# One program for both attentions and the networks between them, with each network twist in two column halves

## The chip, the core and the metric

The kernel runs on one core of a Trainium2 chip. Five engines work side by side: TensorE (PE; matmuls, transposes, and loads of weights, PEld), VectorE (DVE), ScalarE (ACT), GpSimd (POOL) and SyncE (SP), which here issues all DMAs. Each engine takes its own instructions in program order and waits on semaphores that the others raise. The metric is the device time of one execution in microseconds (us); lower is better.

## What is computed

Two layers on x of shape (4, 1024, 128) in float32. Each adds to x the product of an attention s and a gate silu(g). The first attention is full with 16 heads of 8, the second is causal with a bias by position (ALiBi). The first gate comes from a squared-ReLU network and five steps of a spiking neuron; the second from a small coupling network that is run three times over, each time with a "twist" of the state.

```python
    x = L0_attn_x
    xn = _layernorm(x, axis=-1)
    s = _L0_attn_ref(xn, ...)                 # full attention, residual xn
    g = _silu(_L0_ffn_ref(xn, W_fc, W_proj))  # relu^2, W_proj, five spiking steps
    x = x + s * g
    xn = _layernorm(x, axis=-1)
    s = _L1_attn_ref(xn, ...)                 # causal attention with ALiBi
    g = _silu(_L1_ffn_ref(xn, ...))
    x = x + s * g

    def _L1_ffn_ref(x, ...):
        gf = _global_net(x.mean(axis=1, keepdims=True), ...)
        out = x
        for _ in range(NUM_CYCLES):           # 3
            tf = _coupling_net(out, ...)      # gelu, gelu, gelu, sigmoid: 128-128-64-32-1
            combined = 0.7 * gf + 0.3 * tf
            coupling = BASE_COUPLING + adaptive_range * (combined - 0.5) * 2.0
            out = out + coupling * _twist(out)
        return out

    def _twist(x):
        o_r, o_i, p_r, p_i = jnp.split(x, 4, axis=-1)
        return jnp.concatenate([p_r, -p_i, -o_r, o_i], axis=-1)
```

## The kernel before

The kernel is written by hand, engine by engine; the order of the text is the order on each engine. It consists of six programs one behind the other (`prologue`, `row_maxima` for layer 0, `first_attention`, `middle`, `row_maxima` for layer 1, `second_attention`). Each is an `nc.Block()`: at its end all five engines meet at a barrier.

**Attention.** Both attentions go through the batches (4), pairs of head groups, query halves and key tiles in steps. In a step TensorE makes the scores of four heads (128 keys by up to 512 queries each, `a_sc`), ScalarE takes the Exp of them in two instructions of 128x1024 (L979 in the first attention, L1846 in the second), and TensorE multiplies with the values into `a_o` (L1193, L2032). Scores live in three slots of two PSUM banks, the exponentials in a ring of four buffers (`probs`, `RING = 4`), so that step t of ScalarE waits for the product of step t - 4 (`pv_done`). The product of step 0 stands on TensorE behind the scores of step 3. In the second attention GpSimd zeroes the masked triangle of the diagonal steps (L1872) before the product. Before the first product VectorE clears `a_o` (L1155, L1948) and raises `o_clear`; TensorE waits for that ahead of its first score.

**Networks.** `middle` runs the coupling network on x, held transposed in `y` (channels by tokens). Two streams of two batches each take turns: six rounds n = 0 to 5 (stream n mod 2, cycle n // 2). A round on TensorE is `first_layer(n,0)`, `last_layer(n-1)`, `first_layer(n,1)`, `second_layer(n,0)`, `second_layer(n,1)`, `third_layer(n)` (lines 1585, 1613, 1585, 1592, 1592, 1600); ScalarE takes the Gelus (L1397) and, behind the last layer, the Tanhs of the sigmoid (L1418), one of 128x1024 for each of the stream's two batches k. The twist of a batch is three VectorE instructions over all 1024 columns: two of 64 partitions (L1517), each making one half of the rows of `change` from the other half of the state, and one of 128 partitions (L1520) that adds it to the state:

```python
for dst, src in ((low_half, high_half), (high_half, low_half)):
    ins = nc.vector.scalar_tensor_tensor(moved[dst, :], t[src, :], offset[...], out[src, :], ALU.add, ALU.mult)
links.after(ins)
nc.vector.scalar_tensor_tensor(out, moved, slope[:, 0:1], out, ALU.mult, ALU.add).then_inc(twisted[z], 1)
```

`first_layer(n,k)`, two matmuls of 512 columns, waits for the whole twist of round n-2. In rounds 0 and 1 `middle` also does the second half of batch 3 ("31" in the names), which the first attention left over: its output projection (L1654), update and normalization on VectorE (L1541 to L816; L1541 is the first of them), its transpose (L1632), and the queries and keys of both halves. The queries, keys, values and norms of the half "31" (L1636, L1640, L1647) are made in round 5; VectorE makes from the norms the flag (L1569 to L1575) that says whether the second attention needs exact row maxima. With these inputs it doesn't, so `row_maxima` of layer 1 loads the flag on TensorE, VectorE and SyncE, and each jumps over its body. VectorE starts `middle` with some twenty small instructions on constants (L1502 to L1539). In front of its first Gelu and behind its last Tanh ScalarE loads another function table (ACT_TABLE_LOAD at L1446 and L1477).

## Time and profile before

| | us |
|---|---|
| median of 3 runs (916.01 to 917.1) | 916.91 |
| the profiled execution | 914.3 |
| its span from first to last instruction | 912.6 |
| ACT busy in the span | 829.2 (91%) |
| PE busy in the span | 780.9 (86%) |
| DVE busy in the span | 395.0 (43%) |
| POOL busy in the span | 210.3 (23%) |
| mean granted TensorE clock, of full speed | 0.975 |

Stages by the timeline, in us from the span's start: prologue to 50.9, first attention from 55.9 (first Exp) to 534.2 (last), networks and what stands between up to 621.8 (first Exp of the second attention), second attention to the end. A busy share is a mean over stages with different limits; in the stage of the networks no engine is full. A row's times are those of one profiled execution, and the end of a matmul is modelled.

### The profile page before, as it was taken

The page shows a single profiled execution, that of the slowest core. Times are in us where ns is not written, and L with a number is a line of the kernel's source. Part 1 is how long each engine was busy: PE and PEld are TensorE (multiplying, and loading weights), DVE is VectorE, ACT ScalarE, POOL GpSimd, SP SyncE. Part 2 cuts the span into 40 slices and gives each one's busy share as a digit, 9 for nine tenths or more (in the row PEclk, how much of TensorE's full clock was granted, in tenths as well). Part 3 has the DMA queues.
Part 4 walks back from the last instruction along what each step waited for, and adds up shares of the span by engine and source line. Part 5 has one row for each costly group of instructions (what it writes and reads, how often), then busy time and mean ns, then how long its engine had stood idle before and what let it go on. Part 6 is the DMA issues. An engine that isn't in the chain of part 4 may idle for free. (4 is left out here: it accounts for less than half of the span.)

```text
span 912.6 us, 22160 instructions
## 1 busy us (share of the span) xinstructions
PE 780.9 (86%) x9374; PEld 305.5 (33%) x9374; DVE 395.0 (43%) x862; ACT 829.2 (91%) x919; POOL 210.3 (23%) x259
## 2 busy tenths in 40 slices
PE   3949999899999999998999988755887878878876
PEld 2412434234343343433334333212332323323322
DVE  7821254443747446474444777881120121121122
ACT  7759999999999999999999956656999999999996
POOL 2201110130202212121311112002234334324333
PEclk9969999999999999999999999986999999999999
DMA  6882020200300202103000034010112022022000
GB/s 181 281 280 38 2 75 3 74 2 3 98 25 18 104 2 75 48 2 121 2 2 24 25 90 168 0 47 1 38 38 86 14 74 86 1 87 86 2 13 24
DMA packets 31948, 53.45 MB, mean 59 GB/s; under 512 B 5480, under 2 KB 16360, under 8 KB 31848
## 3 DMA queue, kind: packets, MB, share of 16 engines
q1 hardware_dynamic: 31848, 52.01, 18.2%
q8 instruction: 75, 1.23, 0.6%
q14 instruction: 25, 0.20, 0.1%
HBM read 31.29 MB, written 20.71 MB: 57 GB/s over the span
## 5 line engine op out<-in xcount | busy, mean ns | idle before, releaser
L979 ACT ACTIVATE a_probs<-a_sc 128x1024 f32<-128x1024 f32 x512 | 473.6, 1035 | 10.0 <-PE a_sc L1178 9.7
L1846 ACT ACTIVATE a_probs<-a_sc 128x1024 f32<-128x1024 f32 x288 | 269.6, 1047 | 21.6 <-PE a_sc L1997 17.1
L1193 PE MATMUL a_o<-a_probs,vt 128*18 128x256 f32 (+1 forms) x3072 | 271.3, 456 | 0.0
L1178 PE MATMUL a_sc<-q_st,k_st 32*128 32x512 f32 x1024 | 130.7, 499 | 29.5 <-ACT a_probs L979 23.4
L2032 PE MATMUL a_o<-a_probs,vt 128*18 128x256 f32 (+3 forms) x1856 | 152.7, 437 | 0.7
L1991 PE MATMUL a_sc<-q_st,k_st 32*128 32x512 f32 (+3 forms) x768 | 78.5, 423 | 62.5 <-ACT a_probs L1846 51.1
L1872 POOL TENSOR_SCALAR_AFFINE_SELECT a_probs<-a_probs 128x512 f32<-128x512 f32 x128 | 82.8, 666 | 189.9 <-ACT a_probs L1846 189.9
L1193 PEld LDWEIGHTS a_o<-a_probs,vt 128*18 128x18 f32 x3072 | 65.2, 97 | 142.9 <-issue 102.7
L1178 PEld LDWEIGHTS a_sc<-q_st,k_st 32*128 32x128 f32 x1024 | 50.6, 183 | 145.4 <-ACT a_probs L979 135.4
L1006 POOL TENSOR_TENSOR early<-early 128x512 f32<-128x512 f32 x32 | 38.4, 1200 | 176.9 <-DVE early L1116 176.9
L1991 PEld LDWEIGHTS a_sc<-q_st,k_st 32*128 32x128 f32 x768 | 37.1, 185 | 123.8 <-ACT a_probs L1846 106.5
L1905 DVE STREAM_TRANSPOSE a_turn<-a_o 128x512 f32<-128x512 f32 x15 | 10.8, 717 | 152.9 <-PE a_o L2032 152.9
L2032 PEld LDWEIGHTS a_o<-a_probs,vt 128*18 128x18 f32 x1856 | 40.6, 97 | 69.4 <-issue 51.2
L1116 DVE TENSOR_SCALAR early<-a_side 128x512 f32<-128x512 f32 x32 | 22.1, 691 | 67.0 <-PE a_side L112 67.0
L1120 DVE TENSOR_SCALAR y<-a_side,rho 128x128 f32<-128x128 f32 x32 | 9.0, 345 | 92.5 <-PE a_side L112 92.5
L992 POOL TENSOR_TENSOR early<-early,y 128x512 f32<-128x512 f32 x7 | 10.6, 1513 | 144.5 <-DVE early L1131 144.5
L1397 ACT ACTIVATE n_h<-n_ps,cn_b 128x1024 f32<-128x1024 f32 (+1 forms) x24 | 24.1, 1006 | 20.5 <-PE n_ps L1585 10.3
L1517 DVE SCALAR_TENSOR_TENSOR early<-n_th,n_offset,y 64x1024 f32<-64x1024 f32 x24 | 30.8, 1285 | 8.6 <-ACT n_th L1418 8.2
L1014 POOL TENSOR_TENSOR a_square<-parts 128x512 bf16<-128x512 f32 x12 | 15.1, 1258 | 82.7 <-DVE parts L1148 82.7
L112 PE MATMUL a_side<-proj_t,early 128*32 128x128 f32 x1024 | 33.8, 273 | 0.0
L112 PE MATMUL a_side<-y,fc_t 128*32 128x512 f32 x256 | 33.3, 592 | 0.0
L112 PEld LDWEIGHTS a_side<-proj_t,early 128*32 128x32 f32 x1024 | 29.3, 110 | 5.8
(236 smaller groups left out, 712.9 us busy)
## 6 DMA issues: line engine op xcount, KB each, us to landing
q_st<-q_hl SPq DMA_DIRECT2D x48, 256.0 KB
k_st<-k_hl SPq DMA_DIRECT2D x48, 256.0 KB
q_hl<-parts SPq DMA_DIRECT2D x12, 512.0 KB, 4.3
k_hl<-parts SPq DMA_DIRECT2D x12, 512.0 KB, 4.5
q_hl<-early SPq DMA_DIRECT2D x4, 512.0 KB, 4.8
k_hl<-early SPq DMA_DIRECT2D x4, 512.0 KB, 5.3
out_dram<-x SPq DMA_DIRECT2D x7, 256.0 KB, 4.3
x<-in_L_attn_x_dram SPq DMA_DIRECT2D x3, 512.0 KB, 5.9
```

What stands on the lines that cost most here:

```text
L112: ins = nc.tensor.matmul(out[c:c + COLUMN, :], weight[:, c:c + COLUMN], rows, start=start, stop=stop, tile_position=(0, c))
L979: nc.scalar.activation(probs[t % RING][:, 2 * pair:2 * pair + 2, :], scores[unit % SLOTS][:, :, :], ACT.Exp).then_inc(expd, 1)
L1006: pool.tensor_tensor(hidden[f], hidden[f], hidden[f], ALU.mult).then_inc(hid_rdy, 1)
L1116: ins = nc.vector.tensor_scalar_max(hidden[hf[1]], side[:, :], 0.0)
L1178: ins = nc.tensor.matmul(scores[(2 * t + i // 2) % SLOTS][:, i % 2, :], k_st[part, g, kt * P:(kt + 1) * P], q_st[part, g, qh * HALF:(qh + ...
L1193: ins = nc.tensor.matmul(o_ps[32 * h:32 * h + 2 * W9, c0:c1], vt[b % 2][:, kt, gp, h, W9 * gs:W9 * gs + 2 * W9], probs[t % RING][:, h, c0: ...
L1397: nc.scalar.activation(out, source, ACT.Gelu, bias=bias[:, 0:1]).then_inc(squashed[z], 1)
L1517: ins = nc.vector.scalar_tensor_tensor(moved[dst, :], t[src, :], offset[src, 2 * z + k:2 * z + k + 1], out[src, :], ALU.add, ALU.mult)
L1846: nc.scalar.activation(probs[t % RING][:, 2 * pair:2 * pair + 2, :], scores[unit % SLOTS][:, :, :], ACT.Exp).then_inc(expd, 1)
L1872: ins = pool.affine_select(out=part, in_=part, compare_op=ALU.is_ge, fill=0.0, base=0, pattern=[[0, G], [1, P]], channel_multiplier=-1)
L1991: ins = nc.tensor.matmul(banks[i][:, at:at + w], k_st[part, 2 * gp + gs, kt * P:(kt + 1) * P], q_st[part, 2 * gp + gs, qh * HALF + q0:qh * ...
L2032: ins = nc.tensor.matmul(o_ps[32 * h:32 * h + 2 * W9, q0:q0 + w], vt[b % 2][:, kt, gp, h, W9 * gs:W9 * gs + 2 * W9], probs[t % RING][:, h, ...
```

## The change

`first_attention`, `middle`, `row_maxima` of layer 1 and `second_attention` no longer have blocks of their own: a new function `attentions` makes one block in which each engine runs through the four parts one behind the other. Prologue and `row_maxima` of layer 0 stay as they are, with their barriers. What the three barriers kept apart is now kept by semaphores: the networks start on counts of the first attention (`attended`), the second attention on counts of the networks (`freed`, `twisted`, `o_clear`, `drained`). Buffers are shared: one ring of four serves as `probs` in both attentions and in between as the networks' `h1`, `h2`, `h3` and the Tanh of stream 0; the eight PSUM banks are cut differently by each part.

Within the networks:
- Each twist is done in two halves of 512 columns, six instructions in place of three, and each of the two matmuls of `first_layer` waits for its own half.
- The projection of the half "31" moves behind the transpose and `first_layer(0,1)` on TensorE.
- The queries and keys of "31" move from round 5 to rounds 2 and 3; ScalarE writes both a raw copy and the high part (two Identity instructions in place of one), and VectorE subtracts from the raw copy. The norms move to round 4, the flag's last steps to round 5, ahead of the last three twists. The values of "31" move into the second attention as one more piece of side work (`fill("v", B - 1, 1, 3)`).
- VectorE jumps over the body of `row_maxima` between the twists (4,1) and (5,0), and clears `o_ps` between (5,0) and (5,1). TensorE jumps right behind its last layer, and the first product, not the first score, waits for `o_clear`.
- ScalarE waits ahead of step 2 of the second attention for the last twist of stream 0, whose Tanh lies in ring buffer 2.

```diff
@@ first_attention @@
+    room["attended"] = {"scored": (scored, 2 * S), "pv_done": (pv_done, S), "side_in": (side_in, len(fills)),
+                        "xs1_rdy": (xs1_rdy, 2 * B - 1), "skip_rdy": (skip_rdy, 2 * B), "gated": (gated, 2 * B),
+                        "on_rdy": (on_rdy, 2 * B), "o_free": (o_free, B * ENDS), "slots": [(expd, 2 * S - n) for n in (2, 1, 0)]}
@@ row_maxima, pe_part; the same in sp_part and dve_part @@
+        if causal:
+            pe.wait_ge(room["flagged"], room["flag_count"])
@@ middle, act_part, behind second_layer(n) @@
-                    if n == ROUNDS - 1:
-                        high(0, 1, pa[:, 0, :])
...
+            if n in (2, 3):
+                copy_and_high(n - 2)
@@ middle, dve_part, twist @@
+            for hf in range(2):
+                cols = slice(HALF * hf, HALF * hf + HALF)
                     for dst, src in ((low_half, high_half), (high_half, low_half)):
-                        ins = nc.vector.scalar_tensor_tensor(moved[dst, :], t[src, :], offset[src, 2 * z + k:2 * z + k + 1],
-                                                             out[src, :], ALU.add, ALU.mult)
+                    ins = nc.vector.scalar_tensor_tensor(moved[dst, cols], t[src, cols], offset[src, 2 * z + k:2 * z + k + 1],
+                                                         out[src, cols], ALU.add, ALU.mult)
                     links.after(ins)
-                    nc.vector.scalar_tensor_tensor(out, moved, slope[:, 0:1], out, ALU.mult, ALU.add).then_inc(twisted[z], 1)
+                nc.vector.scalar_tensor_tensor(out[:, cols], moved[:, cols], slope[:, 0:1], out[:, cols], ALU.mult,
+                                               ALU.add).then_inc(twisted[z], 1)
@@ middle, pe_part, first_layer @@
-                    if n >= 2:
-                        pe.wait_ge(twisted[z], batch_count(n - 2, k))
                     for hf in range(2):
+                if n >= 2:
+                    pe.wait_ge(twisted[z], half_count(n - 2, k, hf))
@@ middle, pe_part, behind second_layer(n, 1) @@
+            if n in (2, 3):
+                pe.wait_ge(saved, 1)
+                rows_of(n - 2, 1, xt31, ps[n % 2][:, 3, :])
+            if n == 4:
+                norms_of(1, pa[:, 3, :])
...
+        pe.wait_ge(peaks, 2)
                 last_layer(ROUNDS - 1)
@@ second_attention, act_part @@
+            if t == 2:
+                act.wait_ge(twisted[0], 4 * CYCLES)
@@ second_attention, pe_part, score, then product @@
-                pe.wait_ge(o_clear, 1)
...
+                elif unit == SLOTS - 1:
+                    pe.wait_ge(*room["freed"][0])
...
+                if t == 0:
+                    pe.wait_ge(o_clear, 1)
```

On TensorE, at the seam of first attention and networks. Before, `n_ps` is the networks' PSUM and the two branches are the block's end and the barrier:

```order
L1193 MATMUL a_o<-a_probs,vt 18x256 x7
L928 UNCONDITIONAL_BRANCH
L1578 UNCONDITIONAL_BRANCH [waits barrier_Pool_Activation_PE_DVE_SP_release]
L1585 MATMUL n_ps<-y,cn_w 128x512 [waits cn_in]
L1585 MATMUL n_ps<-y,cn_w 128x512
L1654 MATMUL n_ps<-wo_x,on 128x128 x4
L1632 MATMUL n_ps<-ident,xs 128x128 x4
L1585 MATMUL n_ps<-y,cn_w 128x512 x2
```

The same place now; `c_ps` is the PSUM shared by all parts, `c_ring` the shared ring:

```order
L1212 MATMUL c_ps<-c_ring,vt 18x256 x7
L1628 MATMUL c_ps<-y,cn_w 128x512 [waits a0_expd,a0_side_in,cn_in]
L1628 MATMUL c_ps<-y,cn_w 128x512
L1675 MATMUL c_ps<-ident,xs 128x128 [waits a0_expd,a0_xs1_rdy]
L1675 MATMUL c_ps<-ident,xs 128x128 x3
L1628 MATMUL c_ps<-y,cn_w 128x512 x2
L1704 MATMUL c_ps<-wo_x,on 128x128 [waits a0_on_rdy]
L1704 MATMUL c_ps<-wo_x,on 128x128 x3
```

The barrier is gone from between the last product and the first layer, and the projection (L1654, now L1704) stands behind the transposes and the second first layer.

On VectorE, at the end of the networks, before: the twist (4,1), the flag's last steps, the twist (5,1), the block's end, and the flag's load. The clearing of `a_o` (L1948) stands one block further on.

```order
L1520 SCALAR_TENSOR_TENSOR y<-early,n_slope,y 128x1024 [waits n_twist_link]
L1572 COPY n_peak<-n_ps 1x64 [waits n_peak_turned]
L1573 TENSOR_TENSOR n_peak<-n_peak 1x16 [waits n_peaks]
L1574 TENSOR_REDUCE n_peak<-n_peak 1x1 [waits n_peaks]
L1575 TENSOR_SCALAR flag<-n_peak 1x1 [waits n_peaks]
L1517 SCALAR_TENSOR_TENSOR early<-n_th,n_offset,y 64x1024 [waits n_squashed1]
L1517 SCALAR_TENSOR_TENSOR early<-n_th,n_offset,y 64x1024
L1520 SCALAR_TENSOR_TENSOR y<-early,n_slope,y 128x1024 [waits n_twist_link]
L1358 UNCONDITIONAL_BRANCH
L727 UNCONDITIONAL_BRANCH [waits barrier_Pool_Activation_PE_DVE_SP_release]
L729 TENSOR_LOAD flag
```

The same engine now, from the flag's last steps to the jump: between them stands the whole twist (4,1), in halves.

```order
L1611 COPY n_peak<-c_ps 1x64 [waits n_peak_turned]
L1612 TENSOR_TENSOR n_peak<-n_peak 1x16 [waits c_flagged]
L1613 TENSOR_REDUCE n_peak<-n_peak 1x1 [waits c_flagged]
L1614 TENSOR_SCALAR flag<-n_peak 1x1 [waits c_flagged]
L1554 SCALAR_TENSOR_TENSOR early<-c_ring,n_offset,y 64x512 [waits n_squashed0]
L1554 SCALAR_TENSOR_TENSOR early<-c_ring,n_offset,y 64x512
L1557 SCALAR_TENSOR_TENSOR y<-early,n_slope,y 128x512 [waits n_twist_link]
L1554 SCALAR_TENSOR_TENSOR early<-c_ring,n_offset,y 64x512 x2
L1557 SCALAR_TENSOR_TENSOR y<-early,n_slope,y 128x512 [waits n_twist_link]
L748 TENSOR_LOAD flag [waits c_flagged]
```

Behind the jump on VectorE now: the twist (5,0), the clearing of the output bank (`c_ps` at L1619), then the twist (5,1).

```order
L1554 SCALAR_TENSOR_TENSOR early<-c_th,n_offset,y 64x512 [waits n_squashed1]
L1554 SCALAR_TENSOR_TENSOR early<-c_th,n_offset,y 64x512
L1557 SCALAR_TENSOR_TENSOR y<-early,n_slope,y 128x512 [waits n_twist_link]
L1554 SCALAR_TENSOR_TENSOR early<-c_th,n_offset,y 64x512 x2
L1557 SCALAR_TENSOR_TENSOR y<-early,n_slope,y 128x512 [waits n_twist_link]
L1619 MEMSET c_ps 128x512 [waits n_squashed1]
```

Before, one twist stood behind the flag's last steps and none behind the jump; now three and two do.

## Rows read from the trace of the kernel before

**Rows 1.** Busy time by stage: length, PE, PEld, DVE, ACT, POOL, clock, DMA share, GB/s

```profile
560.00:600.00 40.00, 33.69 (x121) 10.03 (x120) 31.29 (x25) 25.49 (x29) 0.00 (x0) 1.00 0.00 1
680.00:900.00 220.00, 181.84 (x2344) 71.59 (x2340) 35.87 (x61) 213.88 (x233) 88.60 (x123) 1.00 0.15 47
```

**Rows 2.** Timeline, seam to networks: start, length, engine, line, out<-in, count [idle before <-releaser]

```profile
532.29 1.94 ACT L979 ACTIVATE a_probs<-a_sc 128x1024 f32<-128x1024 f32 x2
...
533.40 2.09 PE L1193 MATMUL a_o<-a_probs,vt 128*18 128x512 f32 x24
...
537.81 0.65 DVE L1071 SCALAR_TENSOR_TENSOR y<-ext,y 128x512 f32<-128x512 f32 x1
...
538.79 0.16 DVE L1502 TENSOR_REDUCE n_mean<-xn_sums 128x2 f32<-128x4 f32 x1 [0.33 <-PEq L928]
538.79 3.60 PE L1585 MATMUL n_ps<-y,cn_w 128*128 128x512 f32 x4 [3.29 <-PEq L928]
...
541.33 0.16 DVE L1539 TENSOR_SCALAR n_half_b<-cn_scalars 128x2 f32<-128x2 f32 x1
...
542.18 1.15 PE L1654 MATMUL n_ps<-wo_x,on 128*128 128x128 f32 x8
...
543.37 0.69 DVE L1541 TENSOR_TENSOR early<-n_ps,xn 128x512 f32<-128x512 f32 x1 [1.87 <-PE n_ps L1654]
...
553.17 1.98 PE L1585 MATMUL n_ps<-y,cn_w 128*128 128x512 f32 x4
```

**Rows 3.** Timeline of rounds 3 to 5 of the networks

```profile
577.37 1.98 PE L1585 MATMUL n_ps<-y,cn_w 128*128 128x512 f32 x4
...
578.65 2.58 DVE L1517 SCALAR_TENSOR_TENSOR early<-n_th,n_offset,y 64x1024 f32<-64x1024 f32 x2 [1.71 <-ACT n_th L1418]
...
585.19 1.28 DVE L1520 SCALAR_TENSOR_TENSOR y<-early,n_slope,y 128x1024 f32<-128x1024 f32 x1
...
585.90 1.14 PE L1613 MATMUL n_ps<-n_h,n_w_all 32*128 32x512 f32 x8
...
586.97 1.98 PE L1585 MATMUL n_ps<-y,cn_w 128*128 128x512 f32 x4
...
592.58 1.08 PE L1600 MATMUL n_ps<-n_h,cn_w 128*64 128x512 f32 x4 [1.22 <-ACT n_h L1397]
```

**Rows 4.** VectorE by line and shape: count, busy us, mean ns, idle before

```profile
L1060 DVE SCALAR_TENSOR_TENSOR ext<-y 128x512 f32<-128x512 f32 x8 | 10.6, 1320 | 0.3
...
L1071 DVE SCALAR_TENSOR_TENSOR y<-ext,y 128x512 f32<-128x512 f32 x8 | 5.4, 671 | 0.0
```

**Rows 5.** Timeline from round 5 to the second attention

```profile
602.85 1.08 PE L1600 MATMUL n_ps<-n_h,cn_w 128*64 128x512 f32 x4 [0.16 <-ACT n_h L1397]
...
604.94 1.14 PE L1613 MATMUL n_ps<-n_h,n_w_all 32*128 32x512 f32 x8
...
606.15 2.12 ACT L1418 ACTIVATE n_th<-n_ps,n_half_b 128x1024 f32<-128x1024 f32 x2 [1.49 <-PE n_ps L1613]
...
608.29 1.28 ACT L1477 ACT_TABLE_LOAD   x1
...
609.58 0.20 ACT L1477 ACTIVATE n_warm<-n_half_b 128x2 f32<-128x2 f32 x1
...
616.86 1.28 DVE L1520 SCALAR_TENSOR_TENSOR y<-early,n_slope,y 128x1024 f32<-128x1024 f32 x1
620.19 0.48 DVE L1948 MEMSET a_o<- 128x512 f32 x1 [2.04 <-PEq L679]
...
620.73 0.80 PE L1991 MATMUL a_sc<-q_st,k_st 32*128 32x512 f32 x4 [10.80 <-DVE a_o L1948]
...
621.75 1.94 ACT L1846 ACTIVATE a_probs<-a_sc 128x1024 f32<-128x1024 f32 x2 [11.97 <-PE a_sc L1997]
...
632.13 11.20 ACT L1846 ACTIVATE a_probs<-a_sc 128x1024 f32<-128x1024 f32 x12 [1.34 <-PE a_sc L1991]
```

**Rows 6.** Busy time at the second attention's start, columns as in rows 1

```profile
624.00:628.00 4.00, 1.61 (x14) 0.83 (x11) 0.00 (x0) 3.09 (x4) 1.63 (x3) 0.50 0.00 0
```

More of the change, by code:

```diff
@@ L701, in _ @@
[L701 to L702 removed]
+                sp_part(sp)
             @block.tensor
             def _(pe):
[L706 to L723 removed]
@@ new lines, in sb @@
+    def sb(name, shape, dt=F32):
+        return ctx.enter_context(nc.sbuf_tensor(f"a0_{name}", shape, dt))
+    sem = Semaphores(nc, s["ctx"], "a0_")
+    q_st, k_st, vt, parts = s["q_st"], s["k_st"], s["vt"], s["parts"]
+    probs = room["ring"]
+    own, late = (t[:, :, :, :].bitcast(F32).rearrange("p z n t -> p (z n) t") for t in s["early"])
+    hidden = [own[:, f, :] for f in range(FC)]
+    on, xs1, norms = s["on"], s["xs1"], s["norms1"]
+    turn = [late[:, n, :] for n in range(2)]
+    recip = sb("recip", [P, HALF // 32, 2])
@@ new lines, in act_part @@
+    def act_part(act):
+        for t in range(S):
+            b, gp, qh, gs, kt = place(t)
+            if t >= RING:
+                act.wait_ge(pv_done, t - RING + 1)
+            for pair in range(2):
+                unit = 2 * t + pair
+                act.wait_ge(scored, unit + 1)
+                nc.scalar.activation(probs[t % RING][:, 2 * pair:2 * pair + 2, :], scores[unit % SLOTS][:, :, :],
+                                     ACT.Exp).then_inc(expd, 1)
+            for hf, at in ((0, 42), (1, 62)):
+                if t % PER == at:
+                    act.wait_ge(spiked, SPIKE_OPS * (2 * b + hf + 1))
+                    nc.scalar.activation(th[hf][:, :, :], s["y"][:, tiles(b, hf), :], ACT.Tanh,
+                                         scale=GATE_SCALE).then_inc(th_rdy, 1)
@@ L1708 @@
+        pe.wait_ge(peaks, 2)
+        last_layer(ROUNDS - 1)
+        pe.wait_ge(squashed[0], squash_count(ROUNDS - 2, "t1"))
+    room["freed"] = [(squashed[1], squash_count(ROUNDS - 1, f"t{k}")) for k in range(2)]
+    return sp_part, pool_part, act_part, dve_part, pe_part
 LAG1 = 2
@@ new lines, in sp_part, with load, keep @@
+    def sp_part(sp):
+        def load(b, gp):
+            last = PER1 * (b - 1) + PER1 // 2 * (gp + 1) - 1
+            sp.wait_ge(scored, 2 * last + 2)
+            load_pair(sp, s, 1, b, gp, staged[gp])
+        def keep(b, hf):
+            sp.wait_ge(updated, 2 * b + hf + 1)
+            sp.dma_start(out_t[:, tiles(b, hf), :], s["x"][:, tiles(b, hf), :]).then_inc(kept[hf], 16)
+        for hf in range(2):
+            sp.wait_ge(s[f"stored1{hf}"], 32 * B)
+        for b in range(B):
+            if b + 1 < B:
+                load(b + 1, 0)
+            if b > 0:
+                keep(b - 1, 1)
+            if b + 1 < B:
+                load(b + 1, 1)
+            keep(b, 0)
+        for k in range(2):
+            sp.wait_ge(tailed[k], 1)
+            sp.dma_start(out_t[:, tail_tiles(k), :], s["x"][:, tail_tiles(k), :]).then_inc(kept[k], 16)
+        sp.wait_ge(kept[0], 16 * (B + 1))
+        sp.wait_ge(kept[1], 16 * B)
```

2181 lines of the change are left out of this document (1110 added, 1071 removed).

## The prediction

> **What bounds the kernel now.** I read the busy time by stage first. In the second attention ScalarE is busy 213.88 of 220 us, TensorE 181.84 [rows 1]: the Exps are the bound there, and whatever brings the first Exp forward brings the end forward by as much. In the steady part of the networks nobody is full: PE 33.69, DVE 31.29, ACT 25.49 of 40 us [rows 1]. So I looked in the timeline for what waits for what, at three places.
>
> The seam in front. The last Exp ends at 532.29 + 1.94 = 534.23, the last product at 533.40 + 2.09 = 535.49, VectorE at 538.46. Then the barrier: the networks' first layer starts at 538.79, and, TensorE having stood still for 3.3 us, at half clock (3.60 us for what takes 1.98 later) [rows 2].
>
> The rounds. One round is 586.97 - 577.37 = 9.60 us. The twist (2,1) ends at 585.19 + 1.28 = 586.47, and the first layer that needs it starts at 586.97, right behind the last layer at 585.90 + 1.14 = 587.04 (ends are modelled) [rows 3]: it waits for TensorE's own queue, not for the twist.
>
> The seam behind. The last Tanh ends at 606.15 + 2.12 = 608.27; ScalarE has its Exp table at 609.58 + 0.20 = 609.78 and then stands until 621.75. It waits for scores, TensorE for the clearing of `a_o` at 620.19, and VectorE for the barriers behind the last twist, which ended at 616.86 + 1.28 = 618.14 [rows 5].
>
> **The change part by part.** The sum is made against the profiled execution, 914.3 us (span 912.6). It lies 2.6 below the median of 916.91; I carry the gain over in us.
>
> *Front barrier.* TensorE can run on behind its last product: 535.49 + 1.98 (first layer, no pause and so full clock) + at most 1.15 (four transposes; eight rows of such size took 1.15) + 1.98 + 1.15 (projection) = 541.2 to 541.8 [rows 2]. VectorE begins its constants at 538.46 instead of 538.79 and needs 541.49 - 538.79 = 2.70: 541.2 [rows 2]. The chain of the half "31" then starts at 541.2 instead of 543.37, 2.2 us earlier, and round 1 follows it at its old distance (553.17) [rows 2], since its first layer waits for that half's transpose. Bounds: nothing, if that chain is held elsewhere; 3.3, the whole pause of TensorE. I take **2.2**.
>
> *Side work out of round 5.* The third layer comes 602.85 - 592.58 = 10.27 after the one before, 0.67 over a round [rows 3, 5]; the values (L1640), put ahead of the last layer (604.94), add about 0.15. Gone, **0.8**. In rounds 2 and 3 queries and keys lie under the second Gelu, where TensorE waited 1.22 [rows 3]; ScalarE's second copy (some 0.7 us, like a 512-column VectorE instruction) delays the third Gelu, but the last layer that wants it comes only behind a first layer of 1.98 [rows 3]. Zero, 0.5 at most.
>
> *Half twists.* Alone, a 128x512 instruction of this kind takes 0.671 [rows 4]; a twist becomes 6 x 0.67 and two links, about 4.1 us in place of 2.58 + 1.28 = 3.86 [rows 3]. Two twists, 8.2, and 0.7 of the new subtraction fit into 9.60. TensorE's wait by half gains nothing, because the whole twist was ready in time. Zero.
>
> *Rear barriers and order.* VectorE, in old times: twist (4,0) starts at 578.65 + 19.20 = 597.85 and ends at 601.95; four small instructions at 0.16 to 0.2 [rows 2] put the flag at 602.75. TensorE's new waits for it (ahead of the third layer and of the last layer, with both last Tanhs and the whole second attention queued behind) are satisfied, the last layer not being due before 604.1. TensorE's jump follows the last layer; its price is in the 2.04 before the clearing [rows 5], which held two barriers as well, so 0 to 2.04. Even at 2.04 the first score (1.02 from its start to its Exp) is there 3.06 after the last layer, within the two Tanhs and the table load, 2.12 + 1.51 = 3.63 [rows 5]. So the first Exp comes 1.51 behind the last Tanh instead of 621.75 - 608.27 = 13.48 [rows 5]: **12.0**. If the load were not the later of the two it would cost up to 1.
>
> *What is late next.* VectorE still has the twist (4,1) to 606.85, its jump (0 to 2.04), the twist (5,0) and the clearing (0.48): 611.4 to 613.5 in old times, 609.2 to 611.3 after the 2.2. The first product, and behind it on TensorE every score from step 4 on, waits for that. The first Exp is at 609.78 - 0.8 - 2.2 = 606.8; by the program TensorE reaches that product after five Exps, at 0.93 to 1.30 each (the first eight took 632.13 - 621.75 = 10.38) [rows 5]: 611.5 to 613.3. Just in time: zero, with up to 2.5 in the rival below. ScalarE's wait ahead of step 2 (606.85 - 2.2 against 606.8 + 3.7) costs nothing, nor does SyncE's and GpSimd's, whose loads and copies only start earlier. The values of "31" in the second attention are 1.15 of TensorE [rows 2] in a stage where it idles 17%: zero to 0.5.
>
> *Start of the second attention.* It ran at half clock, 0.50 with PE busy 1.61 of 4 [rows 6]; eight Exps took 10.38 where 8 x 0.93 would do. TensorE will again be little used from the last layer on, so I expect the fall again: zero; 1.9 if the clock holds.
>
> Sum: 2.2 + 0.8 + 12.0 = 15.0. Profiled execution 899.3, median **901.9 us**.
>
> **The rivals.**
> *The clock holds.* TensorE stands still 2 us instead of 11, so the first steps may run at full clock. For it: in the rounds 84% busy kept 1.00 [rows 1]. Against: 40% did not lift it [rows 6]. The eight Exps then take some 8.5: 900.0.
>
> *The clearing is late.* The twist (5,0) now shares its time with GpSimd's masks of the first diagonal steps. The same shape with the same kind of operands took 1.320 beside GpSimd and 0.671 alone [rows 4]. If most of its six instructions are so slowed (up to 3.9) and the jump costs its 2.04, the clearing comes 2 to 3.6 after it is wanted, and ScalarE stands for about 2.5: 904.4.
>
> The Trainium skill has both halves of this: "Advanced Engine Details and Errata", GPSIMD Details, says GpSimd shares a read and a write interface with VectorE and conflicts with its instructions that have two SBUF inputs, which every twist instruction has; the rows 1320 and 671 agree. "Runtime: NRT & Kernel Launch", Instruction fetch mechanics, says that a taken branch out of the fetched window stalls until its target is fetched; no row here shows that stall by itself, only the 2.04 that holds it. By both rules the clearing would be late and the time 904.4.
>
> *The front gain is lost.* If the half "31" is held by something other than the barrier (GpSimd's squares fall into its norm chain now), 2.2 go: 904.1.
>
> *VectorE becomes the bound (slower).* A round's twists cost 12p, p being one half instruction. From p = 0.8 they no longer fit into 9.60; at p = 1.10 four rounds lose 4 x 3.6 = 14.4 us and eat the whole gain; at 1.320 [rows 4] four rounds lose 4 x 6.2 = 25: 927. Against it: the 1320 belongs to GpSimd's company, and GpSimd is idle in the rounds, 0.00 of 40 us [rows 1], but for two squares that move there.
>
> **How the numbers follow.** Forecast 901.9: 0.47. Clock holds 900.0: 0.23. Clearing late 904.4: 0.15. Front gain lost 904.1: 0.06. VectorE bound: 0.04. The other 0.05 is what I don't see (a stall in fetching, a wait misread), of which 0.02 within 0.2%, 0.01 slower, 0.02 faster. The range is to hold 901.9, 900.0 and the two of 904, with 1.5 below for a front gain up to 3.3 and 1.6 above: 898.5 to 906. Measurements of this kernel tell 0.2%, about 1.8 us, from no change. Faster 0.47 + 0.23 + 0.15 + 0.06 + 0.02 = 0.93, same 0.02, slower 0.05.
>
> **What would show it.** Right: first Exp of the second attention about 1.5 us behind the last Tanh, and 15 us earlier; rounds of 9.6 us; half instructions of 0.67 to 0.7; first layer of round 0 in 2.0 us; VectorE's first projection step at 541. Wrong: a first product that waits for the clearing with ScalarE idle ahead of the ninth Exp (clearing late); rounds over 10 us with TensorE released by the twist (VectorE bound); a long gap between TensorE's last layer and its first score (the jump).

## The result, and the profile after it

| | before | after |
|---|---|---|
| median, us (lowest to highest, 4 runs each) | 917.0 (916.01 to 917.93) | 905.82 (904.33 to 906.95) |
| profiled execution, us (span) | 914.3 (912.6) | 906.95 (905.2) |
| first layer of round 0 starts | 538.79 | 535.36 |
| first layer of round 1 starts | 553.17 | 551.05 |
| last Tanh ends | 608.27 | 611.38 |
| first Exp of the second attention | 621.75 | 612.80 |

The ratio is 0.9877, 95% interval 0.9859 to 0.9895: faster by 11.2 us. Forecast was a gain of 15.0 (901.9 us); the time lies at the upper end of the range, 898.5 to 906. In this profile the seam in front (553.17 - 551.05 = 2.1 at the first layer of round 1) and the seam behind gave what was forecast; the networks between them became longer, from 608.27 - 553.17 = 55.1 us to 611.38 - 551.05 = 60.3.

The stage table of the changed kernel, columns as in [rows 1]:

```profile
560.00:600.00 40.00, 35.06 (x118) 10.04 (x118) 35.70 (x49) 24.85 (x30) 2.63 (x2) 0.96 0.07 27
680.00:900.00 220.00, 179.87 (x2277) 70.13 (x2274) 36.77 (x65) 209.02 (x227) 82.88 (x115) 0.99 0.15 48
```

VectorE went from 31.29 to 35.70 of 40 us in the networks, and TensorE's clock is no longer 1.00 in either stretch. (The two stretches hold other parts of the program than before, so only the large differences count.)

The front seam in the timeline, to set beside [rows 2]; L1628 is the first layer, L1704 the projection, L1582 the first step of the half "31", L1675 its transposes:

```profile
535.36 1.98 PE L1628 MATMUL c_ps<-y,cn_w 128*128 128x512 f32 x4
...
539.78 0.61 PE L1704 MATMUL c_ps<-wo_x,on 128*128 128x128 f32 x4
...
540.92 0.68 DVE L1582 TENSOR_TENSOR early<-c_ps,xn 128x512 f32<-128x512 f32 x1
...
549.27 0.66 PE L1675 MATMUL c_ps<-ident,xs 128*128 128x128 f32 x4 [2.31 <-DVE xs L839]
...
551.05 3.51 PE L1628 MATMUL c_ps<-y,cn_w 128*128 128x512 f32 x4
...
564.19 3.62 PE L1628 MATMUL c_ps<-y,cn_w 128*128 128x512 f32 x4
```

The first layer starts without a pause and takes 1.98, as long as the later ones at a clock of 1.00; L1582 comes 543.37 - 540.92 = 2.45 earlier. Then TensorE waits 2.31 us for the normalized half, and first layers take 3.51 and 3.62. The same stretches as a table of PE busy time and granted clock (columns: stretch, length, PE busy, clock, DMA share, GB/s) show the clock at these first layers, 0.50 being the lower of the two levels:

```profile
549.00:551.00 2.00, 1.73 (x12) 0.94 0.26 100
551.00:553.00 2.00, 2.00 (x7) 0.50 0.95 351
553.00:555.00 2.00, 2.00 (x9) 0.71 0.52 187
...
565.00:567.00 2.00, 2.00 (x4) 0.50 0.00 0
```

Round 3, which answers to [rows 3]: L1554 are the two instructions of 64 partitions of a half twist, L1557 the one of 128, L1520 the new subtraction, L1407 the squares of the keys or queries on GpSimd:

```profile
575.66 1.59 POOL L1407 TENSOR_TENSOR ext<-parts 128x512 bf16<-128x512 f32 x1 [22.11 <-ACT parts L1463]
576.38 1.41 DVE L1557 SCALAR_TENSOR_TENSOR y<-early,n_slope,y 128x512 f32<-128x512 f32 x1
577.83 1.51 DVE L1554 SCALAR_TENSOR_TENSOR early<-c_th,n_offset,y 64x512 f32<-64x512 f32 x2
579.37 0.75 DVE L1557 SCALAR_TENSOR_TENSOR y<-early,n_slope,y 128x512 f32<-128x512 f32 x1
580.04 0.68 DVE L1520 TENSOR_TENSOR parts<-early,parts 128x512 fp32r<-128x512 f32 x1
580.76 1.51 DVE L1554 SCALAR_TENSOR_TENSOR early<-c_ring,n_offset,y 64x512 f32<-64x512 f32 x2
...
585.42 2.20 DVE L1554 SCALAR_TENSOR_TENSOR early<-c_ring,n_offset,y 64x512 f32<-64x512 f32 x2
```

```profile
578.43 1.13 PE L1628 MATMUL c_ps<-y,cn_w 128*128 128x512 f32 x2
580.18 1.13 PE L1628 MATMUL c_ps<-y,cn_w 128*128 128x512 f32 x2 [0.62 <-DVE y L1557]
...
588.80 1.12 PE L1628 MATMUL c_ps<-y,cn_w 128*128 128x512 f32 x2
590.79 1.12 PE L1628 MATMUL c_ps<-y,cn_w 128*128 128x512 f32 x2 [0.86 <-DVE y L1557]
```

An instruction takes 0.75, not 0.67; beside a square of GpSimd's one took 1.41, and a pair 2.20 in place of 1.51 (the second square runs from 586.02 to 587.06). TensorE now stops in the middle of a first layer until VectorE has the second half. The rounds are 578.43 to 588.80, 10.4 us, and 10.6 to the next (599.41), where they were 9.6.

The rear seam, beside [rows 5]; L1442 is the Tanh, L1619 the clearing, L2087 the first product, L1899 the Exps:

```profile
609.26 2.12 ACT L1442 ACTIVATE c_th<-c_ps,n_half_b 128x1024 f32<-128x1024 f32 x2 [1.34 <-PE c_ps L1656]
611.40 1.28 ACT L1508 ACT_TABLE_LOAD   x1
612.69 0.20 ACT L1508 ACTIVATE n_warm<-n_half_b 128x2 f32<-128x2 f32 x1
612.80 1.92 ACT L1899 ACTIVATE c_ring<-c_ps 128x1024 f32<-128x1024 f32 x2
...
616.89 0.48 DVE L1619 MEMSET c_ps<- 128x512 f32 x1
...
619.93 2.91 PE L2087 MATMUL c_ps<-c_ring,vt 128*18 128x512 f32 x16
...
623.37 7.44 ACT L1899 ACTIVATE c_ring<-c_ps 128x1024 f32<-128x1024 f32 x8 [1.40 <-PE c_ps L2044]
```

The first Exp follows the last Tanh by 612.80 - 611.38 = 1.42 where it was 13.48: 12.06 gained, 12.0 forecast. The clearing is done at 617.37, 2.5 ahead of the first product.

### The profile page after: what moved, and what is told of

The parts are those of the page before. It is cut to its first block, busy times and chain, and to the rows that moved or that the text cites. A ratio compares the mean times of both kernels' runs of the same rounds, so it can differ in the third digit from the quotient of the medians.

```text
span 905.2 us, 22232 instructions
## 1 busy us (share of the span) xinstructions
PE 783.8 (87%) x9398; PEld 305.5 (34%) x9398; DVE 405.5 (45%) x898; ACT 830.3 (92%) x921; POOL 211.7 (23%) x259
## 3 DMA queue, kind: packets, MB, share of 16 engines
HBM read 31.29 MB, written 20.71 MB: 57 GB/s over the span
## 4 chain that ended last, share of the span: by engine, by line
PE 68%; ACT 17%; DVE 5%; issue 3%; ACTq 0%; DVEq 0%
PE c_ps L1212 25%; PE c_ps L1197 13%; ACT c_ring L1899 10%; PE c_ps L2087 10%; PE c_ps L112 10%; PE c_ps L2044 7%; ACT c_ring L1001 5%; DVE early L1554 2%; PE c_ps L1628 1%; DVE y L1557 1%; ACT xs L1906 1%; ACT c_ring L1421 1%; ACT ext L1006 0%; PE c_ps L2050 0%; PE c_ps L1237 0%
## 5 line engine op out<-in xcount | busy, mean ns | idle before, releaser
L1001 ACT ACTIVATE c_ring<-c_ps 128x1024 f32<-128x1024 f32 x512 | 473.6, 1034 | 10.3 <-PE c_ps L1197 10.0
L1899 ACT ACTIVATE c_ring<-c_ps 128x1024 f32<-128x1024 f32 x288 | 269.6, 1048 | 11.3 <-PE c_ps L2050 5.2
L1212 PE MATMUL c_ps<-c_ring,vt 128*18 128x256 f32 (+1 forms) x3072 | 271.7, 457 | 0.0
L1197 PE MATMUL c_ps<-q_st,k_st 32*128 32x512 f32 x1024 | 131.0, 500 | 29.4 <-ACT c_ring L1001 22.9
L2087 PE MATMUL c_ps<-c_ring,vt 128*18 128x256 f32 (+3 forms) x1856 | 154.1, 440 | 0.8 <-DVE ext L1958 0.2
L1924 POOL TENSOR_SCALAR_AFFINE_SELECT c_ring<-c_ring 128x512 f32<-128x512 f32 x128 | 84.1, 676 | 198.7 <-ACT c_ring L1899 198.7
L2044 PE MATMUL c_ps<-q_st,k_st 32*128 32x512 f32 (+3 forms) x768 | 78.6, 424 | 53.9 <-ACT c_ring L1899 53.3
L1212 PEld LDWEIGHTS c_ps<-c_ring,vt 128*18 128x18 f32 x3072 | 65.2, 97 | 143.1 <-issue 102.9
L1197 PEld LDWEIGHTS c_ps<-q_st,k_st 32*128 32x128 f32 x1024 | 50.6, 183 | 145.5 <-ACT c_ring L1001 135.4
L2044 PEld LDWEIGHTS c_ps<-q_st,k_st 32*128 32x128 f32 x768 | 37.1, 185 | 115.8 <-ACT c_ring L1899 104.4
L2087 PEld LDWEIGHTS c_ps<-c_ring,vt 128*18 128x18 f32 x1856 | 40.8, 97 | 70.4 <-issue 51.7
L1013 POOL TENSOR_TENSOR early<-early,y 128x512 f32<-128x512 f32 x7 | 10.6, 1511 | 144.5 <-DVE early L1151 144.5
L112 PE MATMUL c_ps<-proj_t,early 128*32 128x128 f32 x1024 | 33.8, 273 | 0.0
L112 PE MATMUL c_ps<-y,fc_t 128*32 128x512 f32 x256 | 33.3, 592 | 0.0
L1628 PE MATMUL c_ps<-y,cn_w 128*128 128x512 f32 x48 | 27.7, 694 | 3.5 <-DVE y L1557 2.4
```

Source lines behind the costliest of these rows:

```text
L112: ins = nc.tensor.matmul(out[c:c + COLUMN, :], weight[:, c:c + COLUMN], rows, start=start, stop=stop, tile_position=(0, c))
L1001: nc.scalar.activation(probs[t % RING][:, 2 * pair:2 * pair + 2, :], scores[unit % SLOTS][:, :, :], ACT.Exp).then_inc(expd, 1)
L1197: ins = nc.tensor.matmul(scores[(2 * t + i // 2) % SLOTS][:, i % 2, :], k_st[part, g, kt * P:(kt + 1) * P], q_st[part, g, qh * HALF:(qh + ...
L1212: ins = nc.tensor.matmul(o_ps[32 * h:32 * h + 2 * W9, c0:c1], vt[b % 2][:, kt, gp, h, W9 * gs:W9 * gs + 2 * W9], probs[t % RING][:, h, c0: ...
L1628: ins = nc.tensor.matmul(ps[z][:, 2 * k + hf, :], w1[:, :], half(2 * z + k, hf), start=True, stop=True)
L1899: nc.scalar.activation(probs[t % RING][:, 2 * pair:2 * pair + 2, :], scores[unit % SLOTS][:, :, :], ACT.Exp).then_inc(expd, 1)
```

## The experiments

Twelve runs were made in three groups of four, two of them of kernels that had run before; the medians of before were 916.35, 915.98 and 916.08 in them, so times of different groups can be set side by side.

**First group: which part of the change costs what.**

*The changed kernel again.*

> The changed kernel as it is, beside the experiments of this group, to compare them with. Expected: 904.3 to 907 us, ratio to the kernel before 0.988, as measured already. Both theories: the profiled execution shows first layers of the second batch (columns: rounds) 10.4 to 10.6 us apart in rounds 3 to 5.

905.81 us, ratio 0.9895 (0.9874 to 0.9916), 6 runs from 904.12 to 908.55. Its profiled execution (904.96) had the wait of 2.31 and the fall near 549 us, but none near 564, and the same long rounds. So the falls of the clock differ between executions of one program, the long rounds don't.

*The twist whole again.*

```
 def twist(n, k):
-    for hf in range(2):
-        cols = slice(HALF * hf, HALF * hf + HALF)
...
+    for dst, src in ((low_half, high_half), (high_half, low_half)):
+        ins = nc.vector.scalar_tensor_tensor(moved[dst, :], t[src, :], offset[src, 2 * z + k:2 * z + k + 1],
+                                             out[src, :], ALU.add, ALU.mult)
+    links.after(ins)
+    nc.vector.scalar_tensor_tensor(out, moved, slope[:, 0:1], out, ALU.mult, ALU.add).then_inc(twisted[z], 2)
```

> The changed kernel with the twist as it was: three instructions over all 1024 columns, which count two at once, so that every wait stays where it is. Theory A (VectorE became the bound of rounds 3 to 5, because a 512-column instruction takes 0.75 us, more than half of the 1.285 us of a 1024-column one): a twist goes from 4.66 back to 3.9 us, the rounds go back to 9.6 us, and the time falls by 1.5 to 3 us, to 903 to 904.3. Theory B (the missing gain is only that TensorE ran at half clock in rounds 1 and 2): rounds 3 to 5 stay at 10.4 to 10.6 us or the first half of the first layer comes later; the time stays within 0.5 us of the changed kernel or rises by 0.5 to 1.

905.47 us, ratio 0.9881 (0.9859 to 0.9902), 0.3 below the changed kernel: by time, theory B. By the trace, theory A: the Tanhs of the rounds start at 568.01, 577.61, 587.45, 597.05 and 606.65, that is 9.60 to 9.84 apart, and in the changed kernel's repeat at 566.93, 576.53, 586.90, 597.52, 607.24. The rounds gained, and what followed gave it back: the clock was 0.50 from the last layer of round 5 on, and ScalarE's waits behind its eighth Exp were 1.98 and 1.12, where the repeat had one of 1.51. A row of the table by stretches, and ScalarE's timeline:

```profile
606.00:608.00 2.00, 1.23 (x9) 0.50 0.01 4
```

```profile
621.33 4.00 ACT L1896 ACTIVATE c_ring<-c_ps 128x1024 f32<-128x1024 f32 x4 [1.98 <-PE c_ps L2041]
626.45 5.63 ACT L1896 ACTIVATE c_ring<-c_ps 128x1024 f32<-128x1024 f32 x6 [1.12 <-PE c_ps L2041]
```

So neither theory stood alone, and the clock had to be taken out before the twist could be priced: the second group.

*The twist in halves, in the kernel before.*

```
 def twist(n, k):
+    for hf in range(2):
+        cols = slice(HALF * hf, HALF * hf + HALF)
...
 def first_layer(n, k):
-    if n >= 2:
-        pe.wait_ge(twisted[z], batch_count(n - 2, k))
     for hf in range(2):
+        if n >= 2:
+            pe.wait_ge(twisted[z], 4 * ((n - 2) // 2) + 2 * k + hf + 1)
```

> The kernel before with one part of the change alone: the twist in two column halves, with the first layer's waits by half. Theory A (a half costs 0.75 us an instruction): a round then holds 9.3 us of VectorE work against 9.6 us, so the rounds stay near 9.6 to 9.8 us, and the three twists that end the networks put the barrier behind them off by about 2 us in all: 918 to 920 us, ratio 1.001 to 1.004. Theory B (the halves let the first layer start earlier and gain): 914 to 916 us.

918.87 us, ratio 1.003 (1.0016 to 1.0043): slower, as theory A has it. The Tanhs stay 9.60 to 9.71 us apart: two half twists, 2 x 4.66 = 9.3 us, still fit a round. What is too much is the work that the full change adds to a round beside them: a subtraction of 0.68, in round 4 the norm maximum (0.68) too, and the instructions that take 0.7 longer beside GpSimd's squares. What costs here is the end: the first Exp at 623.68 is 15.71 behind the last Tanh (13.48 before), with longer twists ahead of the barrier.

*The front barrier back.* The block is closed behind the first attention, with the order of the work as changed.

```
         with nc.Block() as block:
...
                 first_pe(pe)
+        with nc.Block() as block:
...
                 couple_pe(pe)
```

> The changed kernel with the block of the first attention closed ahead of the networks, as before: the front barrier alone is back. Theory A (the front barrier was worth the 2.1 to 2.45 us by which the first transposes and mixes came earlier): 2 us slower than the changed kernel, 907.5 to 908.5 us. Theory B (the front gain is lost again by the clock falling in rounds 1 and 2, so the barrier costs nothing on balance): within 0.7 us of the changed kernel, and first(2,1) stands where it stands without the barrier.

909.16 us, ratio 0.9924 (0.9906 to 0.9943): 3.35 slower than the changed kernel beside it, more than the 2 of theory A, though the two intervals overlap a little. In its timeline:

```profile
538.33 3.50 PE L1628 MATMUL c_ps<-y,cn_w 128*128 128x512 f32 x4 [3.44 <-PEq L2163]
...
545.02 0.69 DVE L1582 TENSOR_TENSOR early<-c_ps,xn 128x512 f32<-128x512 f32 x1 [4.14 <-PE c_ps L1704]
...
553.37 0.66 PE L1675 MATMUL c_ps<-ident,xs 128*128 128x128 f32 x4 [2.31 <-DVE xs L839]
```

L1582 comes 545.02 - 538.33 = 6.69 behind the first layer, and 543.37 - 538.79 = 4.58 in the kernel before [rows 2], although both have the barrier and a first layer of 3.5 to 3.6 us. It waited for the projection (L1704): that is the new order on TensorE, the projection behind the transposes and `first_layer(0,1)`. So taking away the barrier is worth 3.35 us here and 545.02 - 540.92 = 4.1 at L1582 (1.5 of it the half clock of the first layer), and the new order had taken some 2.1 of that away: about the 2.45 that was left. The wait of 2.31 in front of the transposes is there with the barrier too, and the kernel before had none, so it comes with that order. With the projection first and no barrier the half might start earlier still; that was not tried.

**Second group: TensorE kept busy.** Extra matmuls whose output nothing reads, in places where TensorE waits.

*In front*, where it waited 2.31 us:

```
         global_layer(0, 2, pb[:, 1, :])
+        for _ in range(2):
+            nc.tensor.matmul(pa[:, 3, :], w1[:, :], half(0, 0), start=True, stop=True)
         turn_in(1)
```

> The changed kernel with two extra matmuls of the first layer's shape (0.99 us each at full clock, their output is written over unread) between the last small global layer and the second transposes, where TensorE idled 2.31 us. Theory A (the lost part of the gain is TensorE's fall to half clock that follows this idle stretch): the granted clock stays at 1.00 from 546 to 556 us, first(1,0) takes 1.98 us instead of 2.1 to 3.5, the first layer of round 2 comes 1 to 2 us earlier counted from the first layer of round 0 (31.7 and 33.5 us in the two profiles of the changed kernel), and the time falls by 1 to 2 us to about 904 to 905. Theory B (the fall comes whatever this stretch holds, or VectorE's twists set the pace there): clock or distance unchanged, time within 0.5 us or up to 0.7 us later from the extra work.

906.56 us, ratio 0.9895 (0.9881 to 0.991): no gain. At its place it did what theory A says (the first layer of round 1 starts 550.60 - 535.04 = 15.56 behind that of round 0, 15.69 and 16.96 in the two profiles of the changed kernel, and takes 1.98). Then the clock fell later; TensorE's timeline, the clock of one stretch, and a wait of ScalarE:

```profile
550.60 1.98 PE L1628 MATMUL c_ps<-y,cn_w 128*128 128x512 f32 x4
...
562.25 3.60 PE L1628 MATMUL c_ps<-y,cn_w 128*128 128x512 f32 x4
```

```profile
606.00:608.00 2.00, 1.90 (x12) 0.62 0.01 4
```

```profile
622.58 4.00 ACT L1901 ACTIVATE c_ring<-c_ps 128x1024 f32<-128x1024 f32 x4 [1.98 <-PE c_ps L2046]
```

It fell in round 2, and again near 606 us, and was still 0.50 beyond 622. What one stretch won, the next ones lost.

*At the rear*, in the first three steps of the second attention:

```
+def warm(bank, times):
+    for _ in range(times):
+        nc.tensor.matmul(bank, s["cn"]["w1"][:, :], s["bv1"][:, :, :].rearrange("p t c -> p (t c)"), start=True, stop=True)
...
         score(2 * pair)
+        if pair == 0:
+            pe.wait_ge(*room["freed"][0])
+            warm(scores[2][:, 0, :], 3)
+        if pair == 1:
+            warm(side[:, :], 1)
...
         score(2 * pair + 1)
+        if pair == 0:
+            pe.wait_ge(*room["freed"][1])
+            warm(side[:, :], 1)
```

> The changed kernel with extra matmuls of 512 columns at the start of the second attention, their output written over unread: three behind the first scores, once the bank is free, and one each behind the second and the third scores, where TensorE idled 4.2, 1.2 and 1.3 us. Theory A (my rival that the clock holds: what the half clock costs there is 1 to 1.9 us): the granted clock stays 1.00 from 608 to 624 us, the eight Exps from the first one on take about 9 us instead of 10.4 to 10.6, time 904 to 905. Theory B (the start is bound by the masks on GpSimd and by VectorE's last twists beside them, not by TensorE's clock): the clock holds but the Exps take as long; time within 0.5 us, or up to 0.5 us later.

903.63 us, ratio 0.9865 (0.9848 to 0.9882), 2.2 below the changed kernel (of the first group; the intervals overlap a little): theory A, and a little more than it forecast. ScalarE's timeline and the clock of the stretches, the same stretches of the changed kernel's repeat below:

```profile
611.91 1.92 ACT L1899 ACTIVATE c_ring<-c_ps 128x1024 f32<-128x1024 f32 x2
614.11 1.94 ACT L1899 ACTIVATE c_ring<-c_ps 128x1024 f32<-128x1024 f32 x2 [0.28 <-PE c_ps L2050]
616.24 15.03 ACT L1899 ACTIVATE c_ring<-c_ps 128x1024 f32<-128x1024 f32 x16 [0.18 <-PE c_ps L2044]
```

```profile
608.00:616.00 8.00, 6.39 (x36) 1.00 0.00 1
616.00:624.00 8.00, 6.87 (x85) 1.00 0.01 2
```

```profile
608.00:616.00 8.00, 2.78 (x19) 0.65 0.00 1
616.00:624.00 8.00, 5.90 (x60) 0.71 0.01 2
```

Eight Exps take about 8.1 us (616.24 + 4 x 0.94 - 611.91) and no wait is longer than 0.28; 10.57 in the changed kernel. The masks on GpSimd and the last twists were beside them as before, so they are not what made it 10.57.

*Whole twist and both fillings.*

> The changed kernel with the whole-width twist again and both fillings. If the three losses add up (rounds at 9.6 us, 1.5 us; front clock 1 to 2 us; rear clock 1 to 1.5 us), 901.5 to 903 us, near the 901.9 us of the prediction; if they hide one another, 904 to 905 us.

900.9 us, ratio 0.9831 (0.9815 to 0.9846), and 899.88, 0.9824 (0.9806 to 0.9841), when it ran again in the third group: lower than either forecast. It is the fastest version here, 4.9 and 5.9 below the changed kernel and 15 to 16 below the kernel before. The three edits alone had given 0.3, -0.7 and 2.2, together 1.8; in the profiles of the first two the clock fell near 606 us, and here it did not.

> The whole twist with both fillings once more, beside the three others: 899 to 902 us, ratio 0.983 as before; in its profiled execution the granted clock stays at 1.00 from 546 to 640 us.

The time came as expected. The clock did not: it fell to 0.50 in round 2 (the last section shows it).

*The rear barrier back*, between the networks and the second attention; the row maxima stand ahead of it.

```
-                attend_act(act)
...
+        with nc.Block() as block:
...
+                attend_act(act)
```

> The changed kernel with a block closed between the networks with the row maxima and the second attention: one barrier is back at the rear, but the order of the work is the changed one. Theory A (the rear gain of 12 us is the wait of the first Exp for the last twists and the barrier, not the order of the side work): the first Exp comes about 11 us later than without, at 12 to 14 us behind the last Tanh; 8 to 11 us slower than the changed kernel, 914 to 917 us. Theory B (the barrier itself is cheap and the clearing, the table load and the hoisted branches were what cost): 3 to 6 us slower, 909 to 912 us.

915.09 us, ratio 0.9994 (0.9985 to 1.0002): 9.3 slower than the changed kernel, theory A, and the gain gone: the interval holds 1.

**Third group.**

*One wait in place of that barrier*: the first Exp waits for the last twist.

```
+            if t == 0:
+                act.wait_ge(twisted[1], 4 * CYCLES)
```

> The changed kernel in one block, with one wait added: the first Exp waits for the last twist of the networks, as a barrier would make it, but nothing else waits. Theory A (of the 9.3 us that the rear barrier costs most is this wait, and the barrier's own work is 1 to 2 us): 913 to 914.5 us, the first Exp at 9 to 10 us behind the last Tanh. Theory B (the barrier's own work is most of it): 906 to 910 us.

916.15 us, ratio 0.9994 (0.998 to 1.0008), as much as the barrier, above the 913 to 914.5 of theory A and far from theory B; ScalarE's timeline, first of this kernel, then of the one with the barrier:

```profile
620.41 1.94 ACT L1901 ACTIVATE c_ring<-c_ps 128x1024 f32<-128x1024 f32 x2 [8.89 <-DVE y L1557]
```

```profile
621.23 1.94 ACT L1899 ACTIVATE c_ring<-c_ps 128x1024 f32<-128x1024 f32 x2 [10.22 <-PE c_ps L2050]
```

The first Exp is 10.4 us behind the last Tanh with the wait, 11.7 with the barrier, 1.4 with neither. So 9.0 is the wait for VectorE, which behind the last Tanh still has the two twists (5,0) and (5,1) and the clearing between them, and 1.3 the barrier. The remaining 1.8 (13.5 in the kernel before) is a balance that was not taken apart: there VectorE had other small work, a second barrier and the jumps, but whole twists, which are shorter. By time the wait and the barrier can't be told apart.

*Half twist with both fillings, and whole twist with the rear filling alone.*

> The changed kernel, its twist in halves as it is, with both fillings of TensorE (front and rear). Beside the version with the whole twist and both fillings (900.9 us) it prices the half twist without the clock's falls. Theory A (a half instruction costs 0.75 us and VectorE sets rounds 3 to 5): rounds 4 and 5 stay at 10.4 and 10.6 us, the time is 2 to 3 us above the whole twist, 903 to 904 us. Theory B (the clock's falls are the whole of the missing gain and the rounds have slack): within 0.7 us of it, 900.5 to 901.5.

901.85 us, ratio 0.9847 (0.9828 to 0.9867): 2.0 above the whole twist beside it (899.88), 1.0 above its first run (900.9); the intervals overlap. The distance to the run beside it is the lower end of theory A; the time itself lies between the two forecasts. In the trace the rounds are 10.37 and 10.61, as theory A has them.

> The whole twist and the rear filling, without the front filling. Beside the version with both it prices the front filling when nothing later hides it. Theory A (the fall near 549 us costs 1 to 2 us that reach the end): 902 to 903 us. Theory B (front filling only moves the fall to a later round, as when it was the one edit): within 0.5 us of 900.9.

903.52 us, ratio 0.9857 (0.9837 to 0.9876): 3.6 and 2.6 above the two runs with both fillings, theory A. Its profiled execution was its slowest (906.64), with falls of the clock near 549 and 566 and three more between 630 and 785.

The profiled executions together, in us; the first two distances are worked out from the starts of the first layers of rounds 0 and 1 and the end of the last Tanh. "A" is a fall of the clock between 547 and 555 us, "B" one between 562 and 568. The two kernels with the front barrier begin round 0 at half clock.

```
                        round 0   round 1   last     0 to 1  1 to last  falls
                        starts    starts    Tanh ends          Tanh
before                  538.79    553.17    608.27   14.38    55.10     -
changed                 535.36    551.05    611.38   15.69    60.33     A B
changed, again          535.11    552.07    609.36   16.96    57.29     A
front barrier           538.33    555.03    612.20   16.70    57.17     -
front filled            535.04    550.60    610.01   15.56    59.41     B
rear filled             536.18    552.96    610.49   16.78    57.53     A
half, both filled       535.17    550.73    609.54   15.56    58.81     B
whole                   536.07    552.58    608.77   16.51    56.19     A
whole, rear filled      534.88    551.85    610.04   16.97    58.19     A B
whole, both filled      534.76    550.32    605.20   15.56    54.88     -
whole, both, again      535.26    550.83    607.38   15.57    56.55     B
```

Two executions had a third fall ahead of the last Tanh, near 606: "front filled" and "whole", whose last rounds were 0.6 longer by it (10.32 against 9.72, 9.60 against 8.98). Between executions with the same falls the half twist is 2.3 us longer (57.17 against 54.88, 58.81 against 56.55); B costs 1.6 to 1.7 (58.81 - 57.17, 56.55 - 54.88); A costs about 1 to 1.4 in the first distance (16.5 to 17.0 against 15.56; 0.1 in the changed kernel's first profile, where it came later), and 1.5 to 1.6 more in the second where all of the first layer of round 1 runs at half clock (60.33 - 58.81, 58.19 - 56.55; 3.51 and 3.64 in place of 1.98).

## Why the prediction was right, and where it missed

The direction and the two large terms were right by their mechanism. That 905.82 lies inside the range is in part luck: five of the ten runs of the changed kernel are above 906, and what was lost came mostly from one term put at zero and from falls of the clock that no term held.

**Front barrier, 2.2.** Right: L1582 came 2.45 earlier, the first layer of round 1 2.1 earlier in the first profile, 1.1 in the repeat, and 2.3 to 2.85 where the wait was filled (550.83 to 550.32 against 553.17). The working had the new order in it (projection behind a second first layer); what it did not see is that this order costs 2.1 of the half's start, and that it opens a wait of 2.31 us on TensorE, behind which the clock fell in most executions. Of the rival that GpSimd's squares hold the half, a small part came true: the stretch from L1582 to the end of the normalization took 549.21 - 540.92 = 8.29, with two of its instructions slowed beside squares (0.62 and 1.01), and 551.10 - 543.37 = 7.73 before, with one (0.89).

**Side work out of round 5, 0.8.** Partly: the last two rounds' Tanhs start 603.08 - 594.10 = 8.98 apart in the version with the whole twist and both fillings, 606.15 - 596.71 = 9.44 before, so 0.46. Of that, 0.25 went back between the Tanhs of rounds 2 and 3 (584.50 - 574.65 = 9.85): TensorE waited 0.30 there for a twist instruction that took 1.88 beside a square of GpSimd's, in place of 1.28. In the changed kernel itself the last two are 9.72 apart, with a wait of TensorE of 0.95 for a half twist between them.

**Half twists, zero.** This is the step that failed. It took 0.67 us an instruction from [rows 4] and so 8.2 us for two twists, which with 0.7 of the subtraction fit into 9.60. They took 0.751 each (the median of 24 instructions of L1557):

```profile
L1557 DVE SCALAR_TENSOR_TENSOR y<-early,n_slope,y x24: 750/751/1412, 559.3 to 622.3; 128x512 f32<-128x512 f32 x24
```

that is 9.3 with the links and 10.0 with the subtraction. The rounds came to 10.4 and 10.6, because more was added to them than the subtraction. VectorE ran without a pause from 577.83 to 588.43, 10.60: four half twists of 2.33, the subtraction at 0.60, and 0.68 that one pair took longer beside GpSimd's square. In the next round it was the subtraction, the norm maximum and its small follower (0.79). The prediction named the squares in its rival of a bound VectorE ("but for two squares that move there") and gave them no price. The better row for the twist was at hand: the same instruction over 1024 columns takes 1.28 [rows 3], and 1.28 is not twice 0.67. From 1.284 and 0.751 each 512 columns cost 0.533 and every instruction 0.218 besides; halving a twist doubles that part, 3 x 0.218 more for each and another link. "VectorE: DVE Perf Modes" of the Trainium skill, The TRN2 errata, says that VectorE's instructions with a source in SBUF are slower by a fixed cost per instruction and not by a factor; the trace fits it, with the 0.218. The row 671 was of an instruction with a constant where the twist has one scalar per partition; instructions of 512 columns with such a scalar took 0.74 to 0.75 in the kernel before too ([rows 4] has none of them); that the scalar makes the difference was not tried. Measured, the half twists cost 1.0 to 2.0 us by the medians and 2.3 by the profiles, with the work that moved into the rounds beside them; alone, in the kernel before, they left the rounds at 9.60 to 9.71, and so did that work with the whole twist, but for the 0.25. The rival that VectorE becomes the bound named the mechanism, but put its threshold at 0.8 an instruction, having left the subtraction and the slowed instructions out of it: 12p + 0.60 + 0.68 reaches 9.60 at 0.69.

**Rear barriers and order, 12.0.** Right: 12.06 in the profile, and as the one added wait showed, 9.0 us are what the last two twists and the clearing would cost if the first Exp still waited for them. TensorE's jump is not to be seen: its last layer ends at 608.07 + 1.14 = 609.21, the first score starts at 609.13. VectorE stood for 0.45 between the twist ahead of its jump and the one behind it. So the price of a jump lies at the lower end of 0 to 2.04.

**What is late next.** Right: the clearing was done 2.5 ahead of the first product, which came right behind its scores on TensorE. GpSimd's pair of masks took 2.21 beside the twists and 1.22 alone, and pairs of L1554 1.79 to 2.04 where they take 1.51, so the two do slow each other, but by less than the rival of 904.4 needs; that rival is false.

**Start of the second attention.** As forecast at half clock; the rival in which it holds is false, but its price was about right: 1.9 forecast, 2.2 by the medians when it was made to hold (903.63 against 905.81), 2.5 by the eight Exps (8.1 against 10.57).

**What the sum lacked** is the clock inside the networks and later. Profile against profile, the changed kernel's repeat gained 914.3 - 904.96 = 9.3, 5.7 less than 15.0: 1.1 at the start of round 1 (A), 3.0 from there to the last Tanh (2.3 the half twists, the rest round 5, the squares and 0.1 of clock), 1.6 behind the first Exp. Of the last, some 1.3 is a fall at 846 us that the kernel before did not have; in the changed kernel's first profile, shown here, it stands at 848 (stretches as above):

```profile
846.00:847.00 1.00, 0.29 (x8) 1.00 0.00 0
847.00:848.00 1.00, 1.00 (x13) 0.85 0.08 16
848.00:849.00 1.00, 1.00 (x8) 0.50 0.00 0
```

and ScalarE waits 1.42 us once behind it. That the same fall is missing in others of the changed versions was seen; what sets it off was not found.

## What to carry to other kernels

Price an instruction that is cut in two from the same instruction at its old size, with a fixed part per instruction, and add up the whole round's work on that engine, the moved side work too and what it makes slower, before calling it hidden. Most of this barrier's price was what its slowest engine still had to do, not the barrier: one wait on that engine cost as much. Where TensorE's time hangs on its clock, look at every wait that a new order opens, and price an edit with the clock held: here gains in one stage came back as a slower clock in the next.

## What the runs showed of the hardware

The same program, with the same matmuls in the same order and the same waits, had its clock fall in one execution and not in the other. Round 2 of the whole twist with both fillings, first and second profile (TensorE's timeline):

```profile
561.62 0.38 PE L1666 MATMUL c_ps<-n_gu,n_g_all 32*128 32x2 f32 x2 [0.34 <-ACT n_gu L1470]
561.93 1.98 PE L1625 MATMUL c_ps<-y,cn_w 128*128 128x512 f32 x4
```

```profile
562.13 0.38 PE L1666 MATMUL c_ps<-n_gu,n_g_all 32*128 32x2 f32 x2 [0.34 <-ACT n_gu L1470]
562.44 3.65 PE L1625 MATMUL c_ps<-y,cn_w 128*128 128x512 f32 x4
```

The longest wait of TensorE in the 5 us before was 1.16 us in both. And the kernel with the front barrier had the wait of 2.31 ahead of its transposes and kept its clock (its first layer of round 1 took 1.98; seven other profiles with that wait had the fall behind it). "TensorE: Matmul & The Clock Gate" of the Trainium skill, HAM oscillation, says that a TensorE that waits between its bursts falls back to half its clock; the falls behind the wait of 2.31 agree, the two cases here show that the wait alone doesn't decide it.

The time of a run goes with the mean clock: the ten runs of the changed kernel lie between 904.12 (clock 0.982) and 908.55 (0.971), those of the whole twist with both fillings between 897.27 (0.988) and 901.86 (0.981); a straight line through the ten gives some 0.4 us for 0.001 in both. The spread of one kernel, more than 4 us, is as large as the effects that were to be told apart, which is why the table of profiled executions settles the half twist better than the medians do.
